# Tokens of v and u moved apart, first pair's tokens by TensorE, an earlier gate, half of the prologue's rows on ScalarE, and TensorE's batches without a loop

## Time and profile before

| | |
|---|---|
| median of 3 runs | 1467.37 us |
| profiled execution | 1468.4 us, its span 1466.6 us |
| PE busy | 1389.9 us, 95% of the span |
| DVE busy | 903.6 us, 62% |
| ACT busy | 688.9 us, 47% |
| mean granted TensorE clock | 0.982 of full |
| DMA moved | 51.37 MB |

### The profile page before, as it was taken

One profiled execution on the slowest core, in us unless ns is written; L12 is line 12 of the kernel. 1 busy time (PEld: TensorE's weight loads), 2 busy tenths in 40 slices (PEclk: granted clock), 3 DMA queues, 4 the chain that ended last, 5 costly groups with the idle time before them and its releaser, 6 DMA issues.

```text
span 1466.6 us, 24503 instructions
## 1 busy us (share of the span) xinstructions
PE 1389.9 (95%) x7806; PEld 793.9 (54%) x7806; DVE 903.6 (62%) x1559; ACT 688.9 (47%) x1058; POOL 44.1 (3%) x41
## 2 busy tenths in 40 slices
PE   6999798899998999999999999999999999999968
PEld 3566444455564555555565555555655555555534
DVE  8868443366655665656655656556555666566657
ACT  3556344444443544454444543454544454454421
POOL 4000400000000000000000000000000000000000
PEclk9999899999999999999999999999999999999988
DMA  6012222112221212221112211221212111221110
GB/s 207 1 31 66 43 35 31 26 29 35 30 30 31 33 27 30 36 32 31 26 26 39 36 29 24 36 34 28 30 29 36 32 26 27 38 30 27 25 30 8
DMA packets 302620, 51.37 MB, mean 35 GB/s; under 512 B 280545, under 2 KB 300769, under 8 KB 302465
## 3 DMA queue, kind: packets, MB, share of 16 engines
q1 hardware_dynamic: 302128, 47.82, 19.4%
q0 software_dynamic: 336, 1.64, 0.3%
HBM read 11.64 MB, written 4.19 MB: 11 GB/s over the span
## 4 chain that ended last, share of the span: by engine, by line
issue 85%; DVE 1%; PE 1%; POOL 1%; ACT 0%; POOLq 0%; DVEq 0%
PE psum L1231 1%; DVE arena L917 0%; DVE arena L923 0%; DVE arena L915 0%; POOL u_w_hl L608 0%; POOL v_w_hl L608 0%; POOL rstd_s L623 0%; POOL up_hl L608 0%; DVE arena L939 0%; PE psum L1575 0%; DVE xn_s L663 0%; POOL u_w_hl L605 0%; POOL v_w_hl L605 0%; DVE x_all L932 0%; POOL up_hl L605 0%
## 5 line engine op out<-in xcount | busy, mean ns | idle before, releaser
L1172 ACT ACTIVATE arena<-psum 128x1024 f32<-128x1024 f32 x504 | 476.0, 1030 | 636.5 <-PE psum L1231 636.3
L1231 PE MATMUL psum<-arena 128*64 128x512 f32 x2016 | 466.0, 605 | 26.0 <-DMA arena<-blocks 14.6
L1231 PEld LDWEIGHTS psum<-arena 128*64 128x64 f32 x2016 | 135.0, 138 | 290.0 <-issue 244.7
L1231 PE MATMUL psum<-u_parts,v_parts 64*128 64x512 f32 x1536 | 199.5, 404 | 11.9 <-issue 11.2
L1231 PE MATMUL psum<-v_parts,u_parts 64*128 64x512 f32 (+1 forms) x1568 | 201.9, 397 | 0.0
L866 DVE TENSOR_SCALAR o_hl<-psum,sums 128x512 fp32r<-128x512 f32 x126 | 94.4, 749 | 162.1 <-PE psum L1231 162.1
L1231 PEld LDWEIGHTS psum<-u_parts,v_parts 64*128 64x128 f32 x1536 | 141.7, 187 | 93.1 <-issue 45.3
L1231 PEld LDWEIGHTS psum<-v_parts,u_parts 64*128 64x128 f32 (+1 forms) x1568 | 145.3, 184 | 81.5 <-issue 51.1
L868 DVE SCALAR_TENSOR_TENSOR o_hl<-psum,sums,o_hl 128x512 fp32r<-128x512 f32 x126 | 94.6, 751 | 4.5
L1121 ACT ACTIVATE arena<-psum 128x512 f32<-128x512 f32 x128 | 77.1, 625 | 18.5 <-PE psum L1231 18.5
L923 DVE TENSOR_TENSOR arena<-psum,arena 128x512 f32<-128x512 f32 x96 | 64.6, 689 | 33.7 <-PE psum L1231 31.7
(11 more groups left out here) (211 smaller groups left out, 1517.0 us busy)
## 6 DMA issues: line engine op xcount, KB each, us to landing
arena<-blocks SPq DMA_DIRECT2D x1008, 32.0 KB, 2.0
x_all<-in_x SPq DMA_DIRECT2D x4, 512.0 KB, 5.4
upper<-in_we SPq DMA_DIRECT2D x8, 256.0 KB, 2.7
expert_rows<-upper SPq DMA_DIRECT2D x16, 128.0 KB, 2.5
xn_s<-expert_rows SPq DMA_DIRECT2D x8, 256.0 KB, 2.9
out<-x_all SPq DMA_DIRECT2D x8, 256.0 KB, 2.5
arena<-in_e POOLq DMA_DIRECT2D x1, 896.0 KB, 5.7
arena<-in_wi POOLq DMA_DIRECT2D x1, 576.0 KB, 5.7
```

What stands on the lines that cost most here:

```text
L1172: nc.scalar.activation(th_of(un), psum[:, at:at + 2], ACT.Tanh, scale=0.5 * FACTOR_SCALE ** 2).then_inc(s_th, 2)
L1231: return nc.tensor.matmul(out, lhsT, rhs, start=start, stop=stop)
```

## The change

1. `raw`, `tok` and `blocks`, which held u and v together, become separate tensors. DVE turns v and then u, each by an instruction of half the size. SP moves v by 16 DMAs and then u by 16 (`move_blocks`), each of 32 partitions with 4 runs of 128 bytes. `weighted` waits for v's tokens in the first half of a pair and for u's in the second.
2. Pair 1 of batch 0 has neither turn nor DMAs: PE transposes `u_raw` and `v_raw` (`prep(0, 3, ...)`, `prep(0, 4, ...)`) within the last expert, and ACT copies them (`prep_tok`).
3. The first gate and up products of layer 1's ffn move from half 5 to half 3, behind kq and v; in the tail too.
4. In the prologue DVE normalises the even batches, ACT the odd ones (`odd_rows`, with a shift that DVE computes); PE takes the logits two batches at a time, into two groups of 32 rows, and the exponential becomes two instructions of 32 rows.
5. PE's batches 1 to 7 are written out; the loops of ACT, DVE and SP stay.

```
-FULL_STEPS = {1: [("back", 0)], 2: [("norm", 0)], 3: [("kq", 0), ("v", 0)], 12: [("down", 0)], 15: [("yo", 0), ("yo", 1)]}
-FULL_STEPS |= {h: [("gate", f), ("up", f)] for h, f in ((5, 0), (6, 1), (9, 2))}
+FULL_STEPS = {1: [("back", 0)], 2: [("norm", 0)], 3: [("kq", 0), ("v", 0), ("gate", 0), ("up", 0)], 12: [("down", 0)], 15: [("yo", 0), ("yo", 1)]}
+FULL_STEPS |= {h: [("gate", f), ("up", f)] for h, f in ((6, 1), (9, 2))}
...
-            move_rows(E - 2, E // 2 - 1, 0)
-            move_tokens(0, 0, first_blocks)
-            move_rows(E - 1, E // 2 - 1, 1)
+            for par in range(2):
+                move_rows(E - 2 + par, E // 2 - 1, par)
...
+            def move_blocks(blocks, tok, moved):
+                for r in range(QUARTERS):
+                    for a in range(QUARTERS):
+                        sp.dma_start(tok[32 * r:32 * r + 32, :, 32 * a:32 * a + 32],
+                                     blocks[32 * a:32 * a + 32].rearrange("t (k r c) -> t k r c", k=TB, r=QUARTERS)[:, :, r])\
+                          .then_inc(moved, 16)
+
+            def move_tokens(i, j):
+                sp.wait_ge(s_vb, i * PAIRS + j)
+                move_blocks(v_blocks, v_tok[:, (j + 1) % 2], s_vt[j])
+                sp.wait_ge(s_ub, i * PAIRS + j)
+                move_blocks(u_blocks, u_tok[:, (j + 1) % 2], s_ut[j])
...
             def part_rows(h):
                 dve.wait_ge(s_rstd, h + 1)
-                for n in range(h * X_PART, (h + 1) * X_PART):
-                    if n >= 2:
-                        dve.wait_ge(s_xT, n - 1)
-                    normalised(xn_g[:, n % 2], n, mv1[:, n, :, 0:1], rstd1[:, n].unsqueeze(2)).then_inc(s_xn, 1)
+                odd, even = h * X_PART + 1, h * X_PART
+                nc.vector.scalar_tensor_tensor(shift1[:, odd], mv1[:, odd, :, 0], -1.0, rstd1[:, odd], ALU.mult, ALU.mult)\
+                  .then_inc(s_shift, 1)
+                if h:
+                    dve.wait_ge(s_xT, even - 1)
+                normalised(xn_g[:, 0], even, mv1[:, even, :, 0:1], rstd1[:, even].unsqueeze(2)).then_inc(s_xn, 1)
...
-            def turn(i, j, blocks):
-                if not (isinstance(i, int) and i == j == 0):
-                    dve.wait_ge(s_moved[(j - 1) % PAIRS], (i + (j > 0)) * MOVED)
-                nc.vector.transpose(blocks.rearrange("p w t -> p (w t)"), raw.rearrange("p w t -> p (w t)")).then_inc(s_turned, 1)
+            def turn(i, j, raw, blocks, turned, moved):
+                if not (isinstance(i, int) and i == 0 and j == 1):
+                    dve.wait_ge(moved[(j - 1) % PAIRS], moved_count(i if j else i - 1, (j - 1) % PAIRS))
+                nc.vector.transpose(blocks[:], raw[:]).then_inc(turned, 1)
...
-                        turn(i, j, later_blocks)
+                        turn(i, j, v_raw, v_blocks, s_vb, s_vt)
+                        turn(i, j, u_raw, u_blocks, s_ub, s_ut)
...
+            def odd_rows(n):
+                act.wait_ge(s_shift, n // 2 + 1)
+                if n >= 2:
+                    act.wait_ge(s_xT, n - 1)
+                for k in range(TB):
+                    ins = nc.scalar.activation(xn_g[:, 1, k], x_all[:, n, k], ACT.Identity, bias=shift1[:, n, k:k + 1],
+                                               scale=rstd1[:, n, k:k + 1])
+                ins.then_inc(s_xna, 1)
...
+            def prep_tok(k, tok, bk):
+                act.wait_ge(s_prep_full, prep_index(0, k) + 1)
+                copy(tok[:, 1].rearrange("p k c -> p (k c)"), bk[:]).then_inc(s_prep_free, 1)
...
+            def logits(pair):
+                pe.wait_ge(s_xnT, 2 * pair + 2)
+                for g in range(2):
+                    ins = mm(bank[2][g * 64:g * 64 + 32], wr_b[:, pair * 32:pair * 32 + 32], xn1T[:, 2 * pair + g],
+                             pair == 0, pair == B // 2 - 1)
...
-                if u == 0:
-                    pe.wait_ge(s_moved[(j - 1) % PAIRS], (i + (j > 0)) * MOVED)
+                if blk == 0 and isinstance(i, int) and i == 0 and j == 1:
+                    pe.wait_ge(s_prep_free, prep_index(0, 4) + 1)
+                elif blk == 0:
+                    pe.wait_ge((s_vt, s_ut)[o][(j - 1) % PAIRS], moved_count(i if j else i - 1, (j - 1) % PAIRS))
...
-            pe.wait_ge(s_prep_free, 6)
+            pe.wait_ge(s_prep_free, 8)
             iteration(0, True, False)
-            with pe.Fori(1, B) as i:
+            for i in range(1, B):
                 iteration(i, True, True)
             iteration(B, False, True)
```

More of the change, by code:

```diff
@@ L201, in prep_index, with moved_count @@
 def prep_index(g, k):
[L204 removed]
+    return 3 + k if is_first(g) else g * 2 + 5 + k
+def moved_count(i, j):
+    return (i + (j > 0)) * MOVED
 def is_first(g):
@@ L231, in scatter_bank @@
         def scatter_bank(i):
-            return x_bank(("sc", 0), not isinstance(i, int))
+            return x_bank(("sc", 0), not (isinstance(i, int) and i == 0))
         x_all = sb("x_all", [P, B, TB, D])
@@ L350, in build @@
         at[0] = 0
-        raw = take(2, T)
-        v_raw, u_raw = raw[:, 0], raw[:, 1]
-        tok = take(2, 2 * TB * P).rearrange("p h (w k c) -> p h w k c", w=2, k=TB)
+        u_raw, v_raw = take(T), take(T)
+        u_tok, v_tok = take(2, TB, P), take(2, TB, P)
         th = take(2 * TB, T)
@@ L414, in build @@
         s_us, s_vs_rdy = sem("u_parts_ready"), sem("v_parts_ready")
-        s_turned, s_moved = sem("blocks_turned"), [sem(f"tokens_moved{j}") for j in range(PAIRS)]
+        s_ub, s_vb = sem("u_blocks_turned"), sem("v_blocks_turned")
+        s_ut, s_vt = ([sem(f"{n}_tokens_moved{j}") for j in range(PAIRS)] for n in "uv")
         s_f, s_th, s_out, s_oe = sem("scores_full"), sem("tanh_done"), sem("unit_done"), sem("o_evacuated")
@@ L727, in _ @@
             nc.vector.tensor_tensor(tk_rank, tk_pos, tk_mask, ALU.mult).then_inc(s_tk, 1)
-            rank_of, value_of = (rvT[:, a].rearrange("p k (e b) -> p k e b", e=E) for a in range(2))
+            rank_of, value_of = (rvT[:, a].rearrange("p k (g e b) -> p k g e b", g=2, e=E) for a in range(2))
             def low_rows(n, par):
@@ L1032, in transposed @@
                 copy(xn1T[:, n], bank[par][:]).then_inc(s_xnT, 1)
-            pairs(fori_of(act), transposed)
+            def odd_rows(n):
[6 more added lines that the diff above has]
+                ins.then_inc(s_xna, 1)
+            odd_rows(1)
+            for n in range(0, B, 2):
+                transposed(n, 0)
+                transposed(n + 1, 1)
+                if n + 3 < B:
+                    odd_rows(n + 3)
             act.wait_ge(s_lg, 1)
-            nc.scalar.activation(tk_work, bank[2][0:E * B], ACT.Exp, scale=-1.0).then_inc(s_ex, 1)
+            for g in range(2):
+                ins = nc.scalar.activation(tk_work[g * 32:g * 32 + 32], bank[2][g * 64:g * 64 + 32], ACT.Exp, scale=-1.0)
+            ins.then_inc(s_ex, 1)
             act.wait_ge(s_first, 16 * len(first_consts))
@@ L1117, in prep_raw @@
                     act.wait_ge(s_us if k == 1 else s_vs_rdy, g + 1)
-                    act.wait_ge(s_turned, g)
+                    if isinstance(g, int) and g == 1:
+                        act.wait_ge(s_prep_full, prep_index(0, 4) + 1)
+                    else:
+                        act.wait_ge(s_ub if k == 1 else s_vb, g - 1)
                 if q is not None:
@@ L1233, in _, with transposes @@
             pe.wait_ge(s_first, 16 * len(first_consts))
-            def transposes(n, par):
-                pe.wait_ge(s_xn, n + 1)
-                if later(n):
+            def transposes(n):
+                par = n % 2
+                if par == 0:
+                    pe.wait_ge(s_xn, n // 2 + 1)
+                else:
+                    pe.wait_ge(s_xna, n // 2 + 1)
+                if n >= 2:
                     pe.wait_ge(s_xnT, n - 1)
@@ L1241, in transposes @@
                 ins.then_inc(s_xT, 1)
[L1243 to L1246, removed]
-            pe.wait_ge(s_wr, 2)
[L1248 to L1251, removed]
+            def logits(pair):
+                pe.wait_ge(s_xnT, 2 * pair + 2)
+                for g in range(2):
+                    ins = mm(bank[2][g * 64:g * 64 + 32], wr_b[:, pair * 32:pair * 32 + 32], xn1T[:, 2 * pair + g],
+                             pair == 0, pair == B // 2 - 1)
+                return ins
+            transposes(0)
+            transposes(1)
+            pe.wait_ge(s_wr, 2)
+            for n in range(2, B, 2):
+                transposes(n)
+                transposes(n + 1)
+                logits(n // 2 - 1)
+            logits(B // 2 - 1).then_inc(s_lg, 1)
             def early_prep(w, bk):
@@ L1482, in prep @@
                     ins = product(bk, uv_hl[k - 1], pair, xn1_hl)
+                else:
+                    pe.wait_ge(s_prep_free, prep_index(g, k - 2) + 1)
+                    for t in range(TB):
+                        ins = nc.tensor.transpose(bk[:, t * P:(t + 1) * P], (u_raw if k == 3 else v_raw)[:, t * P:(t + 1) * P],
```

(1 more changed line is left out.)

50 lines of the change are left out of this document (24 added, 26 removed).

## The result

| | before | after |
|---|---|---|
| median | 1466.22 us (4 runs) | 1565.34 us (4 runs, 1563.01 to 1568.81) |
| ratio | | 1.0678 [1.065, 1.0706] |
| span of the profiled execution | 1466.6 us | 1567.0 us |
| mean granted clock | 0.982 | 0.981 |

The account below looks back on a forecast made before the run. PE, busy 95% of the span, was taken as the bound. Terms 10.9 + 14.6 + 7.0 + 2.0 + 3.0 + 1.0 = 38.5 off 1468.4, less 1.0 for the median, gave 1429 us; range 1421 to 1440 alone, 1421 to 1600 with rivals.

Parts of the forecast that it names:

- Moves of v and u apart: SP's token moves: v's 16 transfers first, 0.47 us an issue, so PE's waits for tokens go: -14.6 us (12 to 14.6).
- The first rival: SP's queue becomes the bound, from 0.57 us per issue, 32 issues a pair taking 22.0 us: 1598 us; chance 0.36.
- The third case: SP's queue at 0.57 to 0.61 us per issue: u's tokens a little late in many pairs, about 1480 us; chance 0.06.
- Loop edges: PE's jumps back between batches 1 to 7: written out, the 6 gaps go, -10.9 us (9 to 10.9).
- The cover that I asked about: At the loop edges, PE's scores (3.02 us) and the preps cover the jumps back that DVE and ACT keep.
- Pair 1: Pair 1 of batch 0: without DMAs PE weighs as soon as pv is through, -7.0 us (5.5 to 7.6).
- prologue: Before the first pair: DVE normalises 4 batches fewer, its search starts at 24.6 instead of 27.57, -3.0 us (2 to 4).
- Early gate: Layer 1's ffn: no gain in the batches; in the tail -1.0 us (0.5 slower to 1.5 faster).
- Clock: Windows behind PE's waits with granted clock 0.83: four drops cost 6.8 us in all, -2.0 us expected (0 to 6.8).
- PE's gaps fill up again: At the batch edges ACT and DVE still jump back, tanh next behind the tokens: 1457 us; chance 0.07.

## Why the prediction was wrong

**The step that failed** is the price of an issue under *Moves of v and u apart*: "If all above the floor goes with the runs, 128 runs cost 0.34 + 0.27 / 2 = 0.47 us". It is 0.601, beyond the break-even of 0.57 that the same part worked out. I had read a law out of one coincidence (256 runs in two kinds of transfer), against a row in the same group that contradicted it (512 runs for 0.39), and against the nearest row, 0.61, the same transfer at twice the size. From SBUF to SBUF the shape matters little (0.59 to 0.64 us, 0.70 for 128 partitions with 8 runs); I had compared kinds with different ends, SBUF to SBUF and in or out of HBM, as if size told them apart. The Trainium skill has descriptor generation as "small, variable" (page "DMA: Bandwidth & Descriptors", section on the anatomy of one DMA). That section describes a DMA issued by GpSimd, and these are issued by SP, so it bears on them by likeness only; 0.601 us against 0.611 for twice the size is in line with it.

**The first rival** had the mechanism, and its sum was 33 us too high. A pair took 21.65 us and not 22.0, since an issue costs 0.601 and not 0.611 and the pauses remained: 62 x 0.35 = 22 us. The row loads and stores, which I added (6.5 us), are inside that pace. PE's last weighting of u starts at 1511.88, from there to the end are 55.1 us for the 57.2 that the sum had. With the first issue 0.9 later (167.2 for 166.3) these make 30 of the 33. The rest is that the profiled execution took 1568.8 us, 3.5 above the median.

**The third case**, *SP is just at its limit*, named the very price that came, 0.57 to 0.61 us per issue, and put 1480 us to it, 85 too low. Its step that failed is the pause: 0.04 us between two issues leaves out the longer ones, and from start to start it was 0.677, so 0.076 above the median of an issue. A pair then costs SP 21.65 us against 19.6, and 62 times the difference is 127 us. Nearly as much, 124 us, is between the changed kernel and the one with 24 issues on SP (1.0678 - 0.9829, of 1466).

The other terms, each by the runs that isolate it best:

- *Loop edges*, -10.9: the gaps went, and gave nothing where tokens were late behind them, and 4 to 6 us where few were (1444.06 against 1438.02). The cover that I asked about was of DVE and ACT; the one that mattered was PE's own next wait.
- *Moves apart*, -14.6: with the issues on two queues PE's waits for tokens fall from 25.0 to 8.6 us and the time by 1.1% (0.9938 to 0.9829), 16 us. The aim was sound, and only the queue could not carry it. But v's tokens were late too, against the forecast: 21.0 us of the waits in the changed kernel are for them.
- *Pair 1*, -7.0, and *prologue*, -3.0: together PE's weighting of u starts at 168.20 and not at 174.63 + 3.06 + 0.95 of waiting = 178.6, so 10.4 earlier for 10.0. But the prologue gave 1.45 of it, since ACT's four instructions took 1.64 us (0.41 each, not 0.30) and stood behind two copies. The scores ahead of pair 1's weighting start at 153.74 and not at 157.93, 4.2 earlier, so 2.7 more came before pair 1. From these scores to u's weighting are 14.5 us for 20.7, and 2.40 of the 14.5 are PE's wait for DVE's sums, which the forecast didn't have.
- *Early gate*, -1.0: about 4 us, outside my bounds; the tail alone gave 2.7.
- *Clock*, -2.0: too small. In the kernels with the tokens together and the one with shared queues PE's busy time is 12.9 to 16.3 us less than before for 8 more instructions (1377.0, 1373.8 and 1373.6 against 1389.9), and the granted clock 0.991, 0.994 and 0.995 against 0.982. The profiled execution of before is on the low side there: the runs of that kernel on the first of the three chips had 0.985 to 0.990. In the changed kernel it is paid back: the window from 200 to 250 us (length, busy of PE to POOL, PEclk, DMA), before and after, goes from 1.00 to 0.90, PE being busy for 91% of it and then 83%.

```profile
200.00:250.00 50.00, 45.35 (x260) 24.42 (x257) 19.64 (x30) 22.96 (x33) 0.00 (x0) 1.00 0.21 34
...
200.00:250.00 50.00, 41.55 (x212) 20.54 (x214) 17.52 (x28) 17.62 (x25) 0.00 (x0) 0.90 0.20 31
```

With SP relieved the whole change gives 26 us (1464.16 - 1438.02), where I had 38.5: too much for the loop edges and the prologue, too little for gate and clock. *PE's gaps fill up again* had the effect for the loop edges with the tokens together, and even its time (0.9938 of 1466.22 is 1457 us), but not the cause: it named ACT's tanh, and PE's waits for ACT are 6.5 us there, those for tokens 25.0. Which wait brings which drop of the clock stays open, and so does the 3 us by which the loop was faster.

## What to carry to other kernels

Before splitting a transfer, count the issues of the queue for a period and multiply by the start-to-start time of the nearest row of the same kind (same two memories): 32 x 0.68 against a period of 19.6 decided this case, and a queue that waits 8.6 us in each period can take 12 more such issues, not 16. Relief can come from a second engine's queue; look then at what that engine computes in order behind its moves. And before removing a gap in the bound engine, look at what it waits for just behind: where that was timed by another engine, the gap was worth nothing here, and moving the producer (one block of code, 8 us) was the cheaper way.

## What was not expected of the hardware

- An issue by SP from SBUF to SBUF took 0.590 to 0.629 us for 1 to 16 runs of 128 bytes on 32 partitions, 0.602 to 0.700 for 1 to 8 runs on 128; one from HBM to 32 partitions took 0.432 us, one from 32 partitions to HBM 0.444.
- The issue of a store to HBM from 128 partitions took 0.381 us as the first of eight and 0.87 from the fifth on, 0.404 where it stood alone. So the median of eight issues back to back was twice the price of one.
- POOL's issue of the same transfer (32 partitions, 4 runs) took 0.551 us busy, 1008 times, for 0.601 of SP's.
- A jump back of PE's loop shows as 1.2 to 2.2 us without work; with the moves shared by two queues, these waits were 10.7 us in the trace and 4 to 6 us in the time.
- ACT's normalising of 128 x 128 with a scale and a shift per partition took 0.41 us, the plain copy of that size 0.30.
